# Last token group's routing, sends and shared expert moved within a mixture-of-experts tile loop

## The reference

```python
x = layernorm(x + attention(x))              # 4 causal sequences of 512 tokens, 16 heads
x = layernorm(x + cross_attention(x, ctx))   # mask: query i sees key j only if j % 128 == i
# ffn
shared = silu(x @ sh_up_w + sh_up_b) @ sh_down_w + sh_down_b
scores = softmax(x @ gate_w.T)               # 8 experts
w, i = top_k(scores, 2);  w = w / (w.sum() + 1e-20)
y = sum over the two chosen experts e of w_e * (silu(x @ up_w[e] + up_b[e]) @ down_w[e] + down_b[e])
x = layernorm(x + y + shared)
```

## Time and profile before

| | us |
|---|---|
| three timed runs | 465.94, 466.62, 463.57 (median 465.94) |
| profiled execution, span from first to last instruction | 469.4 |
| first tile's up product (PE) starts | 348.26 |
| last tile's up product starts | 443.85 |
| last result scattered by POOL starts | 450.38 |

### The profile page before, as it was taken

The page is one execution under the profiler, slowest core; times in us unless marked ns, Lnnn a source line. Parts: engine busy times, 40 slices in busy tenths (PEclk is TensorE's granted clock), DMA queues, the critical chain, the costliest instruction groups (busy, mean ns, idle before and its releaser), DMA issues.

```text
span 469.4 us, 11028 instructions
## 1 busy us (share of the span) xinstructions
PE 441.5 (94%) x3645; PEld 396.4 (84%) x3645; DVE 312.6 (67%) x1248; ACT 295.9 (63%) x915; POOL 211.2 (45%) x246
## 2 busy tenths in 40 slices
PE   6999999999999999999999999987998979999971
PEld 5888898988989889899898897977897969999950
DVE  3277676868796656696685869786987343333495
ACT  3578656686576875768667556673544454776555
POOL 1899398430205011302176355742413766666621
PEclk9999999999999999999999999989999979999997
DMA  5950121400400000020022132120124624434775
GB/s 154 308 182 0 61 91 46 137 0 1 136 2 1 1 24 24 25 69 1 0 70 80 52 116 61 34 69 25 45 71 106 179 87 122 128 120 131 240 244 181
DMA packets 26543, 40.16 MB, mean 86 GB/s; under 512 B 3199, under 2 KB 17683, under 8 KB 26483
## 3 DMA queue, kind: packets, MB, share of 16 engines
q1 hardware_dynamic: 21532, 27.86, 19.7%
q0 software_dynamic: 3408, 9.33, 5.6%
q10 hardware_dynamic: 1547, 2.27, 1.7%
HBM read 26.83 MB, written 12.61 MB: 84 GB/s over the span
## 4 chain that ended last, share of the span: by engine, by line
PE 68%; DVE 8%; POOL 8%; issue 5%; DMA 4%; ACT 3%; another core or an unknown queue 1%; SPq 1%; POOLq 0%; ACTq 0%; DVEq 0%
PE bank L301 15%; PE bank L303 14%; PE bank L302 14%; PE bank L818 7%; PE bank L868 6%; PE bank L829 6%; POOL y_dram L625 5%; DMA w_raw<-y_dram 2%; PE bank L771 1%; POOL w_raw L619 1%; PE bank L915 1%; DMA xacc<-in_x_t 1%; ACT probs L1169 1%; DVE probs L1415 1%
## 5 line engine op out<-in xcount | busy, mean ns | idle before, releaser
L1169 ACT ACTIVATE probs<-probs,negmax 128x128 f32<-128x128 f32 x256 | 99.7, 393 | 27.7 <-DVE negmax L1405 27.6
L1405 DVE CUSTOM_DVE_ANT_0 probs<-bank,mask 128x128 f32<-128x128 f32 x256 | 62.7, 284 | 43.2 <-PE bank L818 43.2
L301 PE MATMUL bank<-w_hi,ot_hi 128*128 (+1 forms) x284 | 81.9, 288 | 0.5 <-issue 0.5
L302 PE MATMUL bank<-w_lo,ot_hi 128*128 (+1 forms) x284 | 81.3, 286 | 0.0
L303 PE MATMUL bank<-w_hi,ot_lo 128*128 (+1 forms) x284 | 81.0, 285 | 0.0
L1415 DVE TENSOR_TENSOR probs<-probs,rsum 128x512 f32<-128x512 f32 x64 | 63.1, 985 | 2.2
L301 PE MATMUL bank<-xt_hi,w_hi 128*128 128x512 f32 x144 | 58.7, 408 | 2.0 <-DVE xt_lo L1374 1.1
L602 POOL DMA_INDIRECT xg_dram<-xacc,place x32 | 33.4, 1042 | 57.2 <-PE bank L829 29.6
L625 POOL DMA_INDIRECT y_dram<-qkv,w_raw x39 | 40.5, 1039 | 40.3 <-ACT qkv L1270 39.3
L302 PE MATMUL bank<-xt_lo,w_hi 128*128 128x512 f32 x144 | 56.9, 395 | 0.0
L303 PE MATMUL bank<-xt_hi,w_lo 128*128 128x512 f32 x144 | 56.9, 395 | 0.0
(11 more groups left out here) (230 smaller groups left out, 1051.6 us busy)
## 6 DMA issues: line engine op xcount, KB each, us to landing
qkv<-xg_dram SPq DMA_DIRECT2D x39, 128.5 KB
ex_raw<-in_w_experts SPq DMA_DIRECT2D x18, 256.0 KB
w_raw<-in_w_quads SPq DMA_DIRECT2D x10, 256.0 KB, 4.4
xacc<-in_x SPq DMA_DIRECT2D x4, 512.0 KB, 4.3
ex_raw<-in_w_cross SPq DMA_DIRECT2D x4, 512.0 KB, 4.0
w_raw<-in_ctx_t_in ACTq DMA_DIRECT2D x4, 512.0 KB, 4.0
w_raw<-in_w_quads SPq DMA_DIRECT2D x3, 512.0 KB, 6.8
xacc<-in_x_t SPq DMA_DIRECT2D x3, 512.0 KB, 5.8
```

The lines of the kernel that those rows point to most:

```text
L301: pe.matmul(o, a_hi, b_hi, start=first, stop=False)
L302: pe.matmul(o, a_hi, b_lo, start=False, stop=False)
L1169: nc.scalar.activation(tile, tile, ACT.Exp, scale=-1.0, bias=negmax[:, s.par, h, j:j + 1], accum_out=sums[:, s.par, h, j:j + 1]).then_inc( ...
L1405: nc.vector.tensor_tensor_reduce(probs[:, s.par, h, slices(j, P)], sc_bank[h][:, slices(j, P)], mask[:, :], -SCALE, 3.0e38, ALU.add, ALU.m ...
```

## The change

Nothing of what is computed changes; the order of work and where it is accumulated do.

- PE: `shared_down(2)` is cut in two halves and `route(3)` stands between them; `rank(3)` moves from tile 2 to tile 0. `shared_up(3)` becomes four pieces of 256 tokens by 128 hidden columns, two behind tile 8 and two behind tile 10. `shared_down(3)` leaves the loop: its first half runs behind the last tile, its second half is accumulated straight into the bank that sums group 3's second half.
- ACT: of group 3 only `x2_t` is copied out of PSUM at once; the rounded copies follow at tiles 2 and 3, out of `x2_t`. The exponentials for group 3's weights move from behind the loop to tile 8. The hidden pieces are taken at tiles 9 to 12. `make_scale_last` moves into tiles 25 to 28.
- DVE: `best_two(3)` stands around `tile_x_lo(0)` and ahead of `add_shared(2)`; `places(3)`, `list_later`, `weigh(most)` and `weigh(last_four)` are given out one step behind `tile_x_lo` and two behind `tile_h_lo`. `last_x2_lo` stands at tiles 4 and 5, `last_hidden_lo` at 11 to 13. The first sums of group 0 are no longer given out at tile 36. `add_shared(3)` of the first half only stands behind `moments3(0)`.
- POOL: the sends of group 3 stand before the loop (two) and behind `send_y` of tiles 0, 1 and 2 (two each).

```diff
+PIECES_AT = (8, 8, 10, 10)
-        scale_last = [[th[:, t, slices(c, P)] for c in range(2)] for t in range(2)]
+        scale_last = [[probs_t[:, t, slices(2 * c, P)] for c in range(2)] for t in range(2)]
-        sum_bank = [bank[0], bank[1], bank[4]]
+        sum_bank = [bank[6], bank[7], bank[4]]
+        piece_bank = [bank[6 + n % 2][:, 0:HALF] for n in range(4)]
...
-            last_sends = {5: (0, 1), 6: (2, 3), 8: (4, 5), 9: (6, 7)}
+            last_sends = {0: (2, 3), 1: (4, 5), 2: (6, 7)}
+            for c in range(2):
+                send(G - 1, c)
...
+            def piece_up(n):
+                half, m = divmod(n, 2)
+                if n == 0:
+                    pe.wait_ge(x2_split_last, 2)
+                    pe.wait_ge(logits_taken, G)
+                    pe.wait_ge(place_ready, G)
+                    pe.wait_ge(count_taken, 2)
+                if n >= 2:
+                    pe.wait_ge(silu_done, 2 * (G - 1) + n - 1)
+                here = slice((G - 1) * GROUP + half * HALF, (G - 1) * GROUP + (half + 1) * HALF)
+                for k in range(KT):
+                    c = slice(k * D + m * P, k * D + (m + 1) * P)
+                    mm = three(pe, piece_bank[n], w_hi[:, NE, 0, c], w_lo[:, NE, 0, c],
+                               xt_hi[:, k, here], xt_lo[:, k, here], k == 0, k == KT - 1)
+                mm.then_inc(up_done, 1)
...
-            filler = {2: lambda: rank(G - 1), 9: lambda: shared_up(G - 1), 12: lambda: shared_down(G - 1)}
+            filler = {0: [lambda: rank(G - 1)]}
+            for n, i in enumerate(PIECES_AT):
+                filler.setdefault(i, []).append(lambda n=n: piece_up(n))
             experts = {}
-            shared_down(2)
+            shared_down(2, range(1))
+            route(G - 1)
+            shared_down(2, range(1, 2))
             tile_turn_x(0)
-            route(G - 1)
             tile_turn_x(1)
...
-            pe.wait_ge(th_ready, TILES)
             pe.wait_ge(xg_ready, TILES)
-            pe.wait_ge(shared_added, 2 * G)
+            shared_down(G - 1, range(1))
...
             as_they_are(G - 1, GT // 2)
+            for j in range(GT // 2, GT):
+                shared_down_of(G - 1, j, rows_of(G - 1, j), False, False)
...
+            more = {2: [lambda: last_x2_hi(0)], 3: [lambda: last_x2_hi(1)],
+                    PIECES_AT[0]: [lambda: weights_exp(slice(TOK // P - GT, TOK // P))]}
+            for n, i in enumerate(PIECES_AT):
+                more.setdefault(i + 1, []).append(lambda n=n: piece_silu(n))
+                more.setdefault(i + 2, []).append(lambda n=n: piece_hi(n))
+            for n in range(4):
+                more.setdefault(EARLY + 2 * GT + n, []).append(lambda n=n: make_scale_last(n))
...
-                if i == 9:
-                    shared_hidden(G - 1)
...
-            weights_exp(slice(TOK // P - GT, TOK // P))
...
-            x2_lo(G - 1)
+            parts = best_two(G - 1)
+            drip(parts, 3)
             tile_x_lo(0)
+            flush(parts)
             add_shared(2)
             tile_x_lo(1)
-            parts = best_two(G - 1)
+            parts = places(G - 1)
+            more = {4: [lambda: last_x2_lo(0)], 5: [lambda: last_x2_lo(1)]}
+            for n, i in enumerate(PIECES_AT):
+                more.setdefault(i + 3, []).append(lambda n=n: last_hidden_lo(n))
             for i in range(TILES + 1):
                 if i + 2 < TILES:
                     tile_x_lo(i + 2)
-                    drip(parts, 3)
+                    if i < TILES - 3:
+                        drip(parts, 1)
                 if 0 <= i - 1 < TILES:
                     tile_h_lo(i - 1)
-                    drip(parts, 3)
+                    drip(parts, 2)
                 if i == 1:
                     flush(parts)
-                    parts = iter(())
-                if i == 2:
-                    flush(places(G - 1))
-                    parts = list_later()
-                if i == 9:
+                    parts = itertools.chain(shift_logits(last_four), list_later(), weigh(most))
+                if i == 11:
                     flush(parts)
-                    parts = itertools.chain(weigh(most), shift_logits(last_four))
-                if i == 10:
-                    hidden_lo(G - 1)
-                if i == 13:
+                    parts = weigh(last_four)
+                for then in more.get(i, ()):
+                    then()
+                if i == TILES - 3:
                     flush(parts)
-                    add_shared(G - 1)
-                    parts = iter(())
-                if i == TILES - 3:
                     parts = add_experts(0)
-                if i >= TILES - 3:
-                    drip(parts, {TILES - 3: 3, TILES - 2: 1, TILES - 1: 0, TILES: 0}[i])
             flush(parts)
             flush(moments3(0))
-            weights = weigh(last_four)
-            for n, _ in enumerate(add_experts(G - 2)):
-                if n >= GT:
-                    drip(weights, 2)
-            flush(weights)
+            add_shared(G - 1, range(1))
+            flush(add_experts(G - 2))
```

More of the change, by code:

```diff
@@ L23 @@
 GT = GROUP // P
+HALF = GROUP // 2
 QUADS = HEADS // 4
@@ L943, in shared_up @@
             def shared_up(g):
[L944 to L947, removed]
+                pe.wait_ge(x2_split, 2 * g + 2)
                 if g == 0:
@@ L965, in shared_up, with shared_down_of, shared_down @@
                     mm.then_inc(up_done, 1)
-            def shared_down(g):
-                pe.wait_ge(hid_ready, 2 * g + 2)
+            def piece_up(n):
[13 more added lines that the diff above has]
+                mm.then_inc(up_done, 1)
+            def shared_down_of(g, j, o, first, last):
+                for k in range(KT):
+                    tok = slice(g * GROUP + j * P, g * GROUP + (j + 1) * P)
+                    mm = three(pe, o, xt_hi[:, k, tok], xt_lo[:, k, tok], w_hi[:, NE, 1, slices(k, D)],
+                               w_lo[:, NE, 1, slices(k, D)], first and k == 0, last and k == KT - 1)
+                return mm
+            def shared_down(g, halves=range(2)):
+                if g == G - 1:
+                    pe.wait_ge(hid_ready, 2 * G + 2)
+                else:
+                    pe.wait_ge(hid_ready, 2 * g + 2)
                 if g == 0:
@@ L974, in shared_down @@
                     pe.wait_ge(silu_done, 4)
-                for half in range(2):
+                for half in halves:
                     for j in (2 * half, 2 * half + 1):
[L977 to L981, removed]
+                        mm = shared_down_of(g, j, sdn_bank[g][half][:, slices(j % 2, D)], True, True)
                     mm.then_inc(down_done, 1)
@@ L1078, in _ @@
                     tile_down(i - 2, experts.pop(i - 2))
-                filler.get(i, lambda: None)()
+                for then in filler.get(i, ()):
+                    then()
             def scaled(g, j, c, diagonal):
@@ L1244, in shared_hidden, with last_x2_hi, piece, piece_silu @@
                                          ).then_inc(hid_hi_done, 1)
+            def last_x2_hi(k):
+                nc.scalar.activation(xt_hi[:, k, slices(G - 1, GROUP)], x2_t[:, k, :], ACT.Copy).then_inc(x2_hi_ready, 1)
+            def piece(n):
+                half, m = divmod(n, 2)
+                return m, slice(half * HALF, (half + 1) * HALF)
+            def piece_silu(n):
+                m, here = piece(n)
+                act.wait_ge(up_done, 2 * (G - 1) + n + 1)
+                b = 3 * IT + 2 * NE + m
+                nc.scalar.activation(hid[G - 1][:, m, here], piece_bank[n], ACT.Silu, bias=cols[:, b:b + 1]
+                                     ).then_inc(silu_done, 1)
+            def piece_hi(n):
+                m, here = piece(n)
+                act.wait_ge(silu_done, 2 * (G - 1) + 2 * (n // 2) + 2)
+                nc.scalar.activation(xt_hi[:, m, slices(G - 1, GROUP)][:, here], hid[G - 1][:, m, here], ACT.Copy
+                                     ).then_inc(hid_hi_done, 1)
             def tile_x_hi(i):
@@ L1347, in _ @@
                 square_root(n, g)
-                if n == 0:
-                    make_scale_last()
                 if n == G - 2:
@@ L1729, in wvo_low, with add_shared @@
                                         wvo_hi[:, :, :].bitcast(F32), ALU.subtract).then_inc(wvo_lo_ready, 1)
-            def add_shared(g):
+            def add_shared(g, halves=range(2)):
                 dve.wait_ge(sent[g], 16 * 2 * GT)
-                for half in range(2):
+                for half in halves:
                     dve.wait_ge(down_done, 2 * g + half + 1)
```

45 lines of the change are left out of this document (25 added, 20 removed).

## The result

The changed kernel takes **470.25 us** (median of 4 runs, 468.57 to 471.44); the kernel before took 464.98 in the same comparison (median of 4, 463.57 to 466.62). The ratio is 1.0102 [1.0061, 1.0144]: the change makes the kernel about 1% slower. The forecast was 466.2, no change that can be told, in a range of 459.5 to 470.5. The measured median lies inside that range, by 0.25 us.

What follows compares the result with a forecast made beforehand. PE bounds the dense tiles, with 6.7 us lost between tiles 9 and 13, put down to ACT. Profiled: 469.4 - 1.9 + 0.2 = 467.7; for timed runs 466.2 us, between 464.2 and 467.7, range 459.5 to 470.5.

Steps and rivals of the forecast that it cites:

- The places and the start: Start of the loop: tile 1 at 353.0, places ending about 356.0 against 356.3, tile 6 as now, about 363.3.
- The sends, the term that decides: POOL's queue: early sends delay targets and loads; PE waits 3.1, 1.9 and 1.4 us; tile 13 at 388.6, net -1.9.
- The rival that the sends cost nothing: Loop: earlier places or four buffers carry PE over; tile 13 at 382, total 461.1 or 457.6; chance 0.25.
- ACT's standstill comes back: ACT stands still at another tile without a hole over it: up to +4 on 466.2, 470; chance 0.1.
- the clock rival: PE's half clock holds in the dense stretch, tiles 9 to 13, costing 3.4 us unswallowed: 471.1; chance 0.15.
- The shared up in pieces, -1: Around tiles 9 to 12: PE's cost unchanged, ACT's block of four operations becomes eight smaller ones, saving 1 us.
- The exponentials at tile 8: ACT at tile 8: two table loads, price 2.8 us, hidden from PE; cost 0, or 0.3 to 1 if loads are punctual.
- The shared down product, -2.8: 24 matmuls leave PE's loop before tile 13 and return behind the last tile, hidden by group 3's loads: -2.8 us.
- Behind the loop: After the last tile, DVE: weight operations leave, add_shared and four group 0 sums enter; -0.8 to +0.8, taken as +0.2.
- two readings for the timed runs: Final sum: same difference from the median, 464.2, or no standstill to lose, 467.7; a value between, 466.2, taken.

Runs made afterwards that it cites:

- the kernel with all parts back: Changed kernel with sends, start of the loop and exponentials as before, only the shared-expert edits and dripped list steps left: 468.66 us, ratio 1.0051.
- B2: Kernel before, unchanged, profiled in a further execution without ACT's standstill: time 464.3 us, span 462.6.
- B1: Kernel before, unchanged, the profiled execution that the prediction read, with ACT's standstill: span 469.4 us.
- The kernel with everything together: Changed kernel with targets on DVE, start of the loop as before, five of group 0's sums again in tiles 36 and 37: 461.8 us, ratio 0.992.
- the single padding: Changed kernel with targets ahead of the sends and one padding ahead of each load of tiles 9 to 16: 467.66 us, ratio 1.0034.

## Why the prediction came out as it did

The call, no change that can be told, holds only because the prediction had set that line at 1%, 470.6 us, and the median is 470.25. The interval of the ratio leaves out 1: the kernel did get slower, by 5.3 us, and the forecast lay 0.3 above its own median of before. That the range holds the result, by 0.25 us, is in good part luck; the mechanism of the sends was right, and the step that went wrong is the one from the profiled span to the timed runs, below.

**The places and the start: right.** Tile 1 was forecast 11.9 us after the norm and is at 12.2; `place_ready`, forecast at +14.9, is at 358.05 + 0.16 = +15.0. Tile 0 is 1.0 later than forecast (+9.8 against +8.8). It did not matter: with the start back the time is the same.

**The sends, the term that decides: right, in place and nearly in size.** `target_of(6)` was forecast done at +30.8 and is done at 373.63, +30.4. The waits were forecast as 3.1, 1.9 and 1.4 us in tiles 7, 8 and for tile 12's load; they are 2.46, 0.65 and 0.50, with 0.87 in tile 6 that I had not seen (the load of tile 8, which stands behind `target_of(4)`). Tile 9 is at +36.4 (forecast +36.1), tile 13 at +46.9 (forecast +47.5). Moving only the targets (tile 9 at +31.6), and taking them off POOL (no wait at all, the loss gone), show the cause. The rival that the sends cost nothing is out, and so is the one that ACT's standstill comes back: no wait of ACT in this trace is put down to "remote", as those of the earlier trace rows are.

**The clock: there, and swallowed.** PE was dry for 2.46 us, and the windows of the changed kernel show its half clock, 1.2 of 2.4 GHz, right behind, in the two windows with 0.60 and 0.54:

```profile
370.00:372.00 2.00, 0.00 (x0) 0.00 (x0) 0.29 (x2) 0.38 (x1) 1.70 (x2) 1.00 0.56 135
372.00:374.00 2.00, 1.55 (x7) 1.55 (x8) 0.41 (x2) 0.77 (x2) 1.49 (x4) 0.60 0.69 238
374.00:376.00 2.00, 2.00 (x11) 2.00 (x11) 0.79 (x5) 0.38 (x1) 1.79 (x3) 0.54 0.60 167
376.00:378.00 2.00, 1.35 (x12) 1.15 (x11) 0.17 (x1) 0.97 (x3) 1.76 (x3) 1.00 0.59 194
```

That is at most 1.7 us of PE's pace ((1 - 0.60) x 2 + (1 - 0.54) x 2), half of what the clock rival priced, and PE still waits 0.65 and 0.50 for the next loads, whose times POOL and SP set. So the slow stretch shortens these two waits, forecast 2.15 longer in all, and is swallowed, as the forecast had it; tile 13 is not late. That PE would fall to half clock behind such a hole was no certainty: behind waits of 2.52 (targets ahead of the sends, tile 12's turn) and 2.90 us (sends back, tile 17's turn) the windows show 1.00 throughout, behind the 2.97 of the kernel with all parts back they show 0.50. What makes the difference is not shown. With the targets on DVE there is no hole in tile 7, and the clock is 1.00 in all windows from 366 to 376.

**The shared up in pieces, -1: there, and larger.** From tile 9 to 13 it is 16.03 us in B2 (384.61 - 368.58); less 8.44 for the tiles and 5.6 for the shared products that leaves 2.0 lost, where about 1 was forecast for ACT's block. In the changed kernel it is 10.49 (390.12 - 379.63); less 8.44, 1.41 for two pieces and the wait of 0.50 that leaves 0.1.

**The exponentials at tile 8: right.** Two rows of 1.28 us, no hole of PE behind them but the 0.50 at tile 12's turn, which stands there without them as well, and with them given back the tiles are no faster. By the Trainium skill, ScalarE: Activation LUTs, "What ACT_TABLE_LOAD costs", each switch would take about 2.66 us with its drain; the rows here have 1.28 and the next operation 0.01 us later, so for this case the measurement decides.

**The shared down product, -2.8: gone from the loop, but not free.** In the changed kernel the 2.82 us between tiles 12 and 13 are gone, and behind tile 10 PE waits for no load, as forecast. The cover that I named, the loads of group 3, held for the second half (the last sums of PE wait for nothing); the first half is part of the tail's loss, below. What I did not ask is what the 2.82 us had been hiding in the kernel before: "From tile 17 on the loads need the sends and the padding, all landed by then both before and after" is not so for before, where PE waited 0.56 us in B2. The gain therefore hangs on the sends being early: with all three other parts given back, PE waits 2.97 us at tile 17.

**Behind the loop: +0.2 forecast, +1.1 measured** against B2 (24.1 to 25.2), and -0.3 against B1, whose own tail was 25.6. DVE begins group 2's sums 7.2 us after tile 38's first matmul (450.40 - 443.19) and began them 5.2 after it (443.69 - 438.46) in B2; the timelines of DVE, of after and then of B2:

```profile
449.83 0.66 DVE L1794 TENSOR_TENSOR xacc<-bank,xacc 128x512 f32<-128x512 f32 x1
450.40 1.67 DVE L1855 SCALAR_TENSOR_TENSOR xacc<-w_raw,xacc 128x256 f32<-128x256 f32 x4
```

```profile
443.69 1.67 DVE L1797 SCALAR_TENSOR_TENSOR xacc<-w_raw,xacc 128x256 f32<-128x256 f32 x4 [0.23 <-DMA w_raw<-y_dram]
```

Of these 2.0 us the weights done in the loop give back 0.8. I had counted 0.65 for `add_shared` and had not set it in its queue: it is a DVE operation that waits for PE, ahead of four that don't. Which part of the 2.0 is that order and which the late sums is not settled: with the sums given back the one wait takes the other's place. The kernel with everything together has a tail of 24.5, 0.5 less than with the sums alone. The 0.5 is there already where DVE begins group 2's sums, 6.5 us after tile 38's first matmul (442.04 - 435.51) against 7.0 (450.18 - 443.17); its cause is open. A kernel with `add_shared` behind group 2's sums was not tried.

**From the span to the time: the step that went wrong, and made the forecast 4 us too low.** The sum for the profiled execution was 467.7; the profiled execution after is 468.4. That these are so close is luck in part: the 0.7 between them is made of +2.1 ahead of the norm, -0.6 to tile 13, -0.3 from there to tile 38 and -0.5 in the tail. The prediction had two readings for the timed runs and "took a value between". The second of them (no standstill in timed runs, 467.7 as it is) was the right one, and with the 1.8 us that lie between span and time, which I had left out, it gives 469.5, 0.75 below the measured median. The kernel before had told it: a profiled span 3.5 us above the median of times, when the time is longer than the span, can hardly be a usual execution. ACT's standstill is in that one and in no other trace, so its end was no gain to be shared out.

**What stays open.** Tiles and tail account for 2.9 us of a difference of medians of 5.3. The same two pieces against B2, beside the measured difference of medians, give for the sends back +1.9 (2.0), all three parts back +2.2 (2.3), the sums +3.3 (3.4), the targets on DVE 0.0 (0.8), the same in the kernel before +0.2 (0.1) and the fastest -3.1 (-3.5). They miss by more for the changed kernel (2.4), the exponentials back (+4.3 against 5.7), the start back (+3.3 against 4.5), the targets first (+0.1 against 1.7), with single paddings and the start on top (+2.8 against 1.5) and for the single padding (+5.2 against 1.3). That last execution was the longest of its 12, and a part of the 3.9 is no work of the edit: its clock is 0.50 in the window 348 to 352, and its tile 0 starts at +11.8 instead of +9.8. So a single execution tells a kernel's time to 1 or 2 us, once to no better than 4, and whether the 2.4 are such spread or a slower stage ahead of the norm, the runs don't tell.

## What to carry to other kernels

When an issue moves ahead in an in-order queue, list the smallest things behind it and who waits for them: here 0.3 us operations behind eight sends held the loads, and moving them to another engine (0.2 us there) gave back the whole 1%. Work taken out of a dense stretch is worth what the next-latest chain leaves, so work out that chain's slack before booking the gain (here, with the sends where they were, it had none: PE waited 0.56 us at tile 17 before anything was removed, and a lead of 3.4 us shrank to 1.0 there). Work moved behind the loop joins a queue there: look at what then stands behind it. And before reading a gain out of a profile, set its span against the timed runs: if it is longer than their times, profile again, since its stalls may be that execution's alone.

## What the runs showed of the hardware that was not expected

- One execution of the kernel before had a span of 469.4 us and the next 462.6, with ACT standing 2.54 and 2.58 us ahead of two operations in the first, both put down to "remote", and in neither the second nor any trace of the other kernels.
- The granted clock ahead of the norm differs between executions with no edit to that stage (0.83 and 0.93 in the windows above against 0.91 and 1.00), and the norm's start with it, by 3 us.
- From the end of the last send on POOL to PE's use of a load that waited for it to land it took 4.50, 4.57 and 4.44 us in three kernels, within 0.13 us of each other.
- Waits of PE of nearly one length were followed by the full clock in two kernels (2.52 and 2.90 us, windows of 1.00 behind) and by the half clock in two others (2.46 and 2.97 us, windows of 0.54 and 0.50 behind).
